# Eight output buffers, a tile table written in portions, and a weight load cut in five, in the first expert phase of a four-layer stack

## What is computed

```python
g = jnp.einsum('th,ehi->tei', x, w1)
u = jnp.einsum('th,ehi->tei', x, w3)
act = jax.nn.silu(g) * u
expert_out = jnp.einsum('tei,eih->teh', act, w2)
out = jnp.einsum('teh,te->th', expert_out, scores)
```

## Time and profile before

| what | us |
|---|---|
| median of 3 runs | 1810.74 (1809.96 to 1812.17) |
| the profiled execution | 1807.37 |
| its span on the core | 1805.5 |
| PE busy in the span | 1688.2 (93%) |
| DVE busy | 1149.0 (64%) |
| POOL busy | 912.8 (51%) |

### The profile page before, as it was taken

How to read it: one execution, slowest core, us unless ns; L and a number is a source line. 1 busy time by engine, 2 the same in 40 slices (tenths; PEclk the granted TensorE clock), 3 DMA queues, 4 the chain that set the end, 5 groups by cost and what they waited for, 6 DMA issues and landing times. The chain is left out here.

```text
span 1805.5 us, 38557 instructions
## 1 busy us (share of the span) xinstructions
PE 1688.2 (93%) x11984; PEld 1312.4 (73%) x12029; DVE 1149.0 (64%) x3410; ACT 974.7 (54%) x2775; POOL 912.8 (51%) x1088
## 2 busy tenths in 40 slices
PE   7999689989789999999999999999988999979997
PEld 4787468868646777777777777768867888847765
DVE  4787665638656666666666676457875453347765
ACT  4677245534335566566655666457761455536661
POOL 2366565545446555655565555134765344466610
PEclk9999899999999999999999999999999999999999
DMA  4233275565020000000000000022435344342101
GB/s 159 86 105 116 87 245 165 166 210 179 28 93 1 1 1 1 1 2 1 1 1 2 1 1 1 1 80 90 145 125 180 97 126 131 112 154 79 39 7 47
DMA packets 74549, 138.47 MB, mean 77 GB/s; under 512 B 11568, under 2 KB 56880, under 8 KB 71920
## 3 DMA queue, kind: packets, MB, share of 16 engines
q1 hardware_dynamic: 60624, 96.40, 17.1%
q0 software_dynamic: 13728, 39.60, 6.3%
HBM read 85.14 MB, written 50.82 MB: 75 GB/s over the span
## 5 line engine op out<-in xcount | busy, mean ns | idle before, releaser
L1404 POOL TENSOR_TENSOR L1f_rn<-L1f_ss,L1f_root_c 128x8 f32<-128x8 f32 x64 | 105.5, 1649 | 201.6 <-DVE L1f_ss L1710 199.3
L1537 PE MATMUL L1f_psQ<-L1f_xT,arena 128*128 128x128 f32 x1408 | 168.1, 275 | 0.9 <-ACT L1f_xT L1618 0.9
L1537 PEld LDWEIGHTS L1f_psQ<-L1f_xT,arena 128*128 128x128 f32 x1408 | 165.0, 192 | 3.0 <-ACT L1f_xT L1618 1.1
L2028 POOL DMA_INDIRECT outs_L2f<-L2f_tiles_ys,L2f_tiles_spot x79 | 75.7, 959 | 121.6 <-ACT L2f_tiles_ys L2172 116.1
L1419 POOL TENSOR_TENSOR L1f_rot<-L1f_qn,L1f_sinT 128x512 f32<-128x512 f32 x64 | 113.2, 1788 | 29.2 <-DVE L1f_qn L1726 29.2
L1636 ACT ACTIVATE L1f_sg<-L1f_psQ,vec1f 128x128 f32<-128x128 f32 x192 | 63.4, 364 | 119.0 <-PE L1f_psQ L1537 118.0
L1464 PE MATMUL L1f_psQ<-arena,L1f_hT 128*128 128x512 f32 x256 | 118.4, 605 | 0.6 <-ACT L1f_hT L1625 0.6
L1756 DVE SCALAR_TENSOR_TENSOR L1f_hid<-L1f_psQ,vec1f,L1f_sg 128x128 f32<-128x128 f32 x192 | 61.4, 346 | 78.1 <-ACT L1f_sg L1636 76.8
L2028 POOL DMA_INDIRECT outs_L0f<-L0f_tiles_ys,L0f_tiles_spot x79 | 75.8, 959 | 54.9 <-ACT L0f_tiles_ys L2172 49.0
L1549 PE MATMUL L1f_psB<-arena,L1f_hid 128*128 128x256 f32 (+1 forms) x384 | 99.8, 388 | 0.0
L1409 POOL TENSOR_TENSOR L1f_pr<-L1f_pr,L1f_rs 128x512 f32<-128x512 f32 x64 | 95.6, 1514 | 6.8 <-DVE L1f_rs L1720 6.8
(11 more groups left out here) (545 smaller groups left out, 4664.0 us busy)
## 6 DMA issues: line engine op xcount, KB each, us to landing
L0f_tiles_xs<-rows_L0f SPq DMA_DIRECT2D x79, 144.0 KB
L2f_tiles_xs<-rows_L2f SPq DMA_DIRECT2D x79, 144.0 KB, 2.2
arena<-in_w_L2f SPq DMA_DIRECT2D x8, 1120.0 KB, 5.6
arena<-in_w_L1f SPq DMA_DIRECT2D x8, 1088.0 KB, 7.4
L1x_got<-outs_L0f SPq DMA_DIRECT2D x16, 512.0 KB, 4.2
L3x_got<-outs_L2f SPq DMA_DIRECT2D x16, 512.0 KB, 3.4
arena<-in_w_L0f SPq DMA_DIRECT2D x8, 768.0 KB, 4.8
rows_L0f<-zero SPq DMA_DIRECT2D x31, 144.0 KB
```

Source lines behind the costliest of these rows:

```text
L1404: nc.gpsimd.tensor_tensor(rn[:, s.p, h], ss[:, s.p, h], root_c[:, 0:LH], ALU.pow).then_inc(s_rn, 1)
L1537: mm = nc.tensor.matmul(out, w, xT[:, k], start=(k == 0), stop=(k == KC - 1), skip_group_check=True)
L2028: nc.gpsimd.indirect_dma_start(r.outs, bass.IndirectOffsetOnAxis(spot[:, t % YR:t % YR + 1], 0), ys[:, t % YR], None).then_inc(r.s_out[t % ...
```

## The change

YR goes from 4 to 8, for both expert phases, with as many semaphores. The owners of the second list are worked out in four portions of 11 or 12 tiles, behind tiles 12, 14, 16 and 18, where one step stood behind tile 12. PE's turning of the table waits only for the links ahead of them (LISTED). The L2x weights go in four column slices of 512 (the last with 6 more) and the bias row as a fifth DMA, each behind the load of tile 40, 45, 50, 55 and 60. The L3x weights are cut in the same way, but all five DMAs are issued at the old place.

```diff
--- before.py
+++ after.py
@@ -66,7 +66,7 @@
 SPARE = TILES - FULL
 C_PAD = C_STEP + TILES
 CONSTS = C_PAD + TILES
-YR = 4
+YR = 8
 BATCHES = tuple((i, 2) for i in range(0, NB - 2, 2)) + ((NB - 2, 1), (NB - 1, 1))
 LASTS = [first + size - 1 for first, size in BATCHES]
 RING = 8
@@ -79,6 +79,9 @@
 
 COLS1X, ROWS1X = 4 * KC, 2 * D
 COLS1F, ROWS1F = 2 * KC + 2 * UNITS1, D + 2 * LD
+
+
+SLICES = {"L0x": 1, "L2x": 4, "L3x": 4}
 
 
 class Step:
@@ -216,7 +219,9 @@
 
         d = self.dram
         if name in ("L0x", "L2x", "L3x"):
-            return [(self.slot[:, 0:HEADS_W + 6], d[f"w_{name}"]),
+            n = HEADS_W // SLICES[name]
+            edges = list(range(0, HEADS_W, n)) + [HEADS_W + 6]
+            return [(self.slot[:, a:b], d[f"w_{name}"][:, a:b]) for a, b in zip(edges, edges[1:])] + [
                     (self.slot[:, HEADS_W + 6:SLOT], d[f"row_{name}"].partition_broadcast(P))]
         if name in ("L0f", "L2f"):
             n = (L0F if name == "L0f" else L2F) // 8
@@ -236,10 +241,11 @@
     def dma(self, eng, name, dst, src):
         eng.dma_start(dst, src).then_inc(self.loaded[name], 16)
 
-    def load(self, eng, name):
-
-        for dst, src in self.parts(name):
-            self.dma(eng, name, dst, src)
+    def load(self, eng, name, only=None):
+
+        for i, (dst, src) in enumerate(self.parts(name)):
+            if only is None or i == only:
+                self.dma(eng, name, dst, src)
 
     def load_in_rounds(self, eng, names, n):
 
@@ -253,7 +259,7 @@
 
     def wait(self, eng, name):
 
-        n = {"L0x": 2, "L2x": 2, "L3x": 2, "L0f": 8, "L2f": 8, "L1f0": 6, "L1f1": 6}.get(name, 3)
+        n = {"L0x": 2, "L2x": 5, "L3x": 5, "L0f": 8, "L2f": 8, "L1f0": 6, "L1f1": 6}.get(name, 3)
         eng.wait_ge(self.loaded[name], 16 * n)
 
 
@@ -1959,7 +1965,9 @@
     GROUPS = G if shared else 0
     READ, REST = r.ready, TILES - r.ready
     TABLE_AT, READ_ONE = 14, 3 if READ else 0
-    ALL_LINKS = TABLE_ROUTE + (READ_ONE + 6 if READ else 0)
+    OWNERS_AT = (12, 14, 16, 18)
+    LISTED = TABLE_ROUTE - 3 + (READ_ONE + 6 if READ else 0)
+    ALL_LINKS = LISTED + 3 * (len(OWNERS_AT) if READ else 1)
     with Phase(nc, r.name + "_tiles") as ph:
         xs, ys = ph.sb("xs", [P, XR, ROW]), ph.sb("ys", [P, YR, D])
         xT, sg, ac, aT = ph.sb("xT", [P, 2, D]), ph.sb("sg", [P, 2, P]), ph.sb("ac", [P, 2, W]), ph.sb("aT", [P, 2, W])
@@ -2014,9 +2022,9 @@
                 sp.dma_start(xs[:, t % XR], r.rows[bass.ds(row, P)]).then_inc(s_x[t % XR], 16)
                 if READ and XR <= t < XR + E:
                     empty(sp, [t - XR])
-                if READ and t == XR + E:
+                if READ and t > READ + XR and t % 5 == 0:
                     for load in loads:
-                        load(sp)
+                        load(sp, t // 5 - (READ + XR) // 5 - 1)
 
         @block.gpsimd
         def _(pool):
@@ -2039,7 +2047,7 @@
             cols = {}
 
             def table(bank):
-                pe.wait_ge(s_tab, ALL_LINKS)
+                pe.wait_ge(s_tab, LISTED)
                 for i in range(2):
                     mm = nc.tensor.transpose(psT[0:1, bank, i * P:(i + 1) * P], tab[:, 4 + i:5 + i], c.ident)
                 mm.then_inc(s_turned, 1)
@@ -2188,8 +2196,8 @@
             dve.wait_ge(r.s_place, 2 * len(BATCHES))
             v.tensor_scalar(r.ends[:, :], r.carry[0:1, len(BATCHES) % 2], -1.0, None, ALU.add).then_inc(s_ends, 1)
 
-            def owners(reached, lo, hi):
-                step = c.consts[:, C_STEP:C_STEP + hi - lo].unsqueeze(2).broadcast_to([P, hi - lo, E])
+            def owners(reached, lo, hi, base):
+                step = c.consts[:, C_STEP + lo - base:C_STEP + hi - base].unsqueeze(2).broadcast_to([P, hi - lo, E])
                 link(v.tensor_tensor(reach[:, lo:hi], reached.unsqueeze(1).broadcast_to([P, hi - lo, E]), step, ALU.is_gt))
                 link(v.tensor_copy(one[:, lo:hi, 0:1], reach[:, lo:hi, 0:1]), wait=False)
                 link(v.tensor_tensor(one[:, lo:hi, 1:], reach[:, lo:hi, 1:], reach[:, lo:hi, 0:E - 1], ALU.subtract), wait=False)
@@ -2231,19 +2239,20 @@
                 link(v.scalar_tensor_tensor(tab[:, 5:6], tab[:, 7:8], tab[:, 6:7], tab[:, 5:6], ALU.mult, ALU.add))
                 link(v.tensor_scalar(tab[:, 4:5], tab[:, 0:1], float(r.unit), None, ALU.mult))
 
-            def tile_owners():
-                owners(run2[:, :], READ, TILES)
-                assert link.n == ALL_LINKS
+            def tile_owners(i, n):
+                lo, hi = (READ + i * (TILES - READ) // n for i in (i, i + 1))
+                owners(run2[:, :], lo, hi, READ)
+                assert i + 1 < n or link.n == ALL_LINKS
 
             if READ:
-                owners(r.reached[:, :], 0, READ)
+                owners(r.reached[:, :], 0, READ, 0)
             else:
                 tile_counts()
                 sums()
                 experts()
                 tile_rows()
                 spare_rows()
-                tile_owners()
+                tile_owners(0, 1)
 
             def table(bank):
                 dve.wait_ge(s_turned, 1)
@@ -2325,8 +2334,8 @@
                     tile_rows()
                 if READ and t == 10:
                     spare_rows()
-                if READ and t == 12:
-                    tile_owners()
+                if READ and t in OWNERS_AT:
+                    tile_owners(OWNERS_AT.index(t), len(OWNERS_AT))
                 if turned_next and t in TURNS:
                     i = TURNS.index(t)
                     if i == 0:
@@ -2344,7 +2353,7 @@
         prepare(nc, c, dram)
 
         def loads(*names):
-            return [lambda sp, n=n: c.load(sp, n) for n in names]
+            return [lambda sp, only=None, n=n: c.load(sp, n, only) for n in names]
         with ExitStack() as first:
             r = Route(nc, first, ctx, "L0f", 1, 0, UNIT_GLU, False, READY)
             heads_attention(nc, c, "L0x", 0, mask=dram["mask"], loads=("L0f", "L1x"), route=r)
```

## The result

| what | before | after |
|---|---|---|
| median of 5 runs, us | 1809.96 (1805.83 to 1812.17) | 1801.03 (1799.15 to 1802.36) |
| ratio to before, 95% interval | | 0.9955 [0.9939, 0.9971] |
| the profiled execution, us | 1807.37 | 1800.39 |
| its span, us | 1805.5 | 1798.3 |

The change makes the kernel 8.9 us faster by the medians and 7.2 us by the spans. The interval of the ratio stands for a gain between 5.3 and 11.0 us. The forecast was 1802.3 with 8.4 us gained. The diff moves the code of expert_tiles down by eight or nine lines: silu is L2166, spot L2305, hidden L2100, turn_in L2088, the load of a tile L2022.

What follows compares the result with a forecast made beforehand. PE was taken to bound the first expert phase, with holes. Gains of 1.6 + 6.76 + 0.45 us, less 0.3 (row write) and 0.1 (load parts), gave 8.4 us off 1810.74: 1802.3 us, range 1799.5 to 1807.0.

Steps and rivals of the forecast that it cites:

- Eight buffers remove the waits for scatters: First expert phase: all 11 DVE waits for scatters, 12.3 us, should go; tiles 9 to 13 gain 1.6 us.
- the table steps: Tiles 9 to 13: DVE's table steps behind tiles 7, 8 and 10 stay and keep 0.45 us of the loss.
- The hole of 6.76 us: Tiles 22 and 23: scatter waits and lower clock go with eight buffers and the L2x load moved; gain 6.76 us.
- Parts of the L2x load: Behind tiles 40 to 60: each quarter delays the next load 1.4 us, which fits; 0.1 us lost for all five.
- rival 3: Tiles 41, 46, 51, 56: load parts delay tile loads beyond their free time, making the kernel slower, 1817.5 us; chance 0.05.
- The free time of a tile load: A tile's load has some 6.0 us from issue to use, 2.2 for landing, so 3.8 us are free.
- Owners in portions: Behind tiles 12 to 18: 0.32 us per large instruction, 3.0 us of DVE work instead of 2.0, cost 0.
- Tile 15: PE's turning of the table and DVE's copy wait for each other; untouched, gain 0, still 1.4 us lost.
- Tile 31 and the last row write: Tile 31's scatter wait goes, gain 0.45 us; last row write delays tile 32's load, issued at 276.1, costing 0.3.
- Rival 1: Tile 31: row-write chain takes over, PE waits up to 2.8 us, gain falls to some 5, 1805.5 us; chance 0.16.
- L3x: Before L2f: three DMAs more, 1.4 us of SP, hidden by 10 us of waiting for row writes; effect nothing.
- The rule on the shared port: DVE operations with two SBUF inputs lock out POOL; could cost up to 1.0 us, but nothing was charged.

Runs made afterwards that it cites:

- yr8_only: The kernel before with eight output buffers instead of four and nothing else: 1807.46 us against 1808.24, ratio 0.9993.
- no_move: The changed kernel with the L2x load back behind tile 22 and the L2x and L3x weights uncut: 1808.02 us, ratio 0.9998 to the kernel before.
- move_only: The changed kernel with four output buffers and owners in one piece, keeping the moved and cut loads: 1804.15 us, ratio 0.9977 to the kernel before.
- both_new_2: The changed kernel with earlier late row writes and the table turned into the other half of psT: 1801.83 us, ratio 0.9953 to the kernel before.
- no_yr8: The changed kernel with four output buffers instead of eight, owners still in portions: 1803.87 us, ratio 0.9975 to the kernel before.
- whole_at_40: The changed kernel with the L2x load uncut, all of it behind the load of tile 40: 1801.53 us, ratio 0.9949 to the kernel before.
- no_portions_2: The changed kernel with the owners in one piece behind tile 12: 1801.27 us against 1811.13 for the kernel before, ratio 0.9947.
- after_again: The changed kernel unchanged, on a slower chip: 1830.89 us, ratio 0.9987 to the kernel before.
- early_rows: The changed kernel with late row writes behind tiles 1, 3, ... 15 instead of 2, 5, ... 23, on the slower chip: 1831.78 us, ratio 0.9991.

## Why the prediction was right, point by point

- **Eight buffers remove the waits for scatters.** Shown: 12.3 us in 11 times to no row at all, and back to 8.9 us in 14 times when the buffers alone are undone. Tiles 9 to 13 gained 2.04 - 0.22 = 1.8 us, predicted 1.6. The 0.45 us left for the table steps was 0.22.
- **The hole of 6.76 us.** The prediction said that with eight buffers alone the load of tile 23 would still be late. Shown: 7.02 and 7.19 us lost with it in the old place. The gain was 6.76, as predicted. The prediction didn't say what each part carries: the move alone takes 4.9 to 6.1 us of it, the buffers alone nothing, and the buffers are needed only for the rest. With the hole the stretch at the lower clock went: the granted clock was 0.66 there in yr8_only and no_move too, with PE standing about 4 us at a time, and 1.00 in move_only, where it never stood so long.
- **Parts of the L2x load.** Predicted 0.1 us lost; measured 0.28 against 0.35 before in tiles 41 to 62, so nothing, and rival 3 with its four late loads didn't come. The estimate of 1.4 us delay for a part wasn't measured by itself.
- **The free time of a tile load.** This step is a figure for some tiles and not for all. I took 6.0 us from issue to use. At tile 40 it is 6.3, so the parts were costed rightly. At tile 22 it was 3.6, and by the 5.5 us of delay measured there I took the whole load for more than tile 40 could hide. It isn't: the delay was 6.5 - 2.2 = 4.3 us, 4.1 were free, and PE waited 0.16.
- **Owners in portions.** Predicted 0.32 us for a large instruction and cost 0; measured 0.32 to 0.40 us, and no loss is seen behind tiles 12 to 18. The reason that I gave for the part, that in one piece it might delay PE, isn't borne out: one piece costs nothing either.
- **Tile 15.** Predicted untouched, 1.4; measured 1.56. The wait is the turning of the table: with the other half of psT and one iteration more it fell to 0.26.
- **Tile 31 and the last row write.** The load of tile 32 was predicted for 276.1 and went out at 275.58; it took 3.1 us and not 2.2, so PE waited 0.49 us, and the tile lost 0.87 in this profile, 0.45, 0.46 and 1.15 in three others with the same row writes. Predicted was 0.3 us of stall in place of the 0.45 that goes, so the term is too small by 0.15 to 0.85 us. The 0.45 was misread as well. The prediction counted it as one of the eleven waits for scatters, but it doesn't go with them: with eight buffers, no wait for a scatter and the L2x load in its old place tile 31 still loses 0.38 (yr8_only) and 0.50 us (no_move). So the gain of 0.45 in the sum isn't borne out. In yr8_only PE stands before hidden of tile 31, right behind the turning of tile 32, for nothing that the profile shows:

```profile
287.02 0.73 PEld L2092 LDWEIGHTS L0f_tiles_psH<-arena,L0f_tiles_xT 128*128 128x128 f32 x4 [0.35 <-issue]
```

The chain, row write, load, PE, stands in the timeline; the one test of it on such a chip, both_new_2 with the row writes earlier, has no loss at tile 31. Since no_yr8 has none either, with the old places, one profile isn't proof. Rival 1, a stall of up to 2.8 us, was of the right kind and too large.

- **L3x.** Predicted nothing. The phase of L2f comes 6.5 us earlier (first tile load at 1384.6, before 1391.1) and is no longer: 173.9 us from the first to the last load, before 174.6. Of the 8.0 us by which silu of tile 78 comes earlier, 1.5 are lost again before L2f and 0.7 gained in it, which gives the 7.2 us of the spans. From silu of tile 78 to the first load of L2f the profiles on the faster chips take 1025.9 to 1029.9 us, in no order of the edits, so that much of a difference between two executions has nothing to do with the change.

```profile
L2022 SPq DMA_DIRECT2D L2f_tiles_xs<-rows_L2f x79: 332/333/346, 1384.6 to 1558.5; - x79
```

- **Tile 20, not foreseen.** The changed kernel loses some 0.5 us there, in two profiles. In the timeline PE's hidden of that tile begins late, after a wait that the profile ties to nothing:

```profile
260.31 1.12 PE L2100 MATMUL L0f_tiles_psH<-arena,L0f_tiles_xT 128*128 x4 [0.27 <-issue]
```

It isn't in whole_at_40 (0.06), which has the same owners, and in no_portions_2, without a portion there, 0.28 us are lost. So the portions don't explain it. This stays open.

By steps: 1.8 and 6.76 us gained, less 0.1 (tile 15), 0.5 (tile 20), 0.4 (tile 31) and 0.1 in small change between, give the 7.43 us to a rounding of tiles 8 to 78. Silu of tile 78 comes 365.22 - 357.19 = 8.0 us earlier; the 0.6 us between was gained before tile 8. The beginning of the phase varies that much by itself: silu of tile 2 lies between 228.80 and 231.10 us in the profiles on the faster chips, in no order of the edits. The forecast's median had 8.4 us of gain for 8.9 measured. That this is so near is in part luck. Between tiles 8 and 78 the sum was 1.0 us too high (8.4 against 7.43): 0.6 us at tile 31, 0.5 at tile 20 and 0.3 at tile 15 and between, less 0.4 that tiles 9 to 13 and the load parts did better. That the medians gained more than the 7.2 us of the two profiled executions is within what executions of one kernel differ by. The main term, the hole, was right by its mechanism and its size.

The rule on the shared port (the Trainium skill, SBUF — State Buffer, "SBUF: two separate sides") is narrower on the page than the prediction has it: an operation with two SBUF inputs counts only against a GpSimd operation that reads SBUF. The scatters read their rows and row numbers from SBUF tiles (ys and spot), so the rule would have shown as longer scatters on POOL beside DVE's comparisons. All 79 scatters of the changed kernel:

```profile
L2036 POOL DMA_INDIRECT outs_L0f<-L0f_tiles_ys,L0f_tiles_spot x79: 954/959/987, 230.9 to 361.4; - x79
```

954 to 987 ns, with a median of 959, leaves no room for an instruction held up for 0.3 us. Four of them ran at the same time as one of the comparisons of 0.34 to 0.40 us, and took 0.95 or 0.96 us. For indirect DMAs on POOL beside such DVE instructions the rule isn't seen here.

## What to carry to other kernels

When a timeline shows a wait, look for the next one that ends at the same place before pricing its removal: here two waits of 4.5 and 3.9 us lay on each other. Taking away the longer one alone, by buffers, gave nothing that could be told (0.02 and 0.07%). Moving the load that causes both gave 0.23 and 0.25%, and with the buffers 0.45%. So look for what the waits have in common, and move that first. A large load that isn't urgent belongs where the loads behind it have the most time between issue and use, and that time is read at the place itself (3.6 us beside the zero writes, 6.3 later in the same loop). With the place right, cutting it made no difference that could be measured.

## What the runs showed that I had not expected

**A chip that is 23 to 30 us slower.** From 600 to 1000 us, the local attention, it works as the others (PE busy 400.00 of 400 us in both). In the expert phase engines stand for times that no wait explains, in the waits of 225 to 375 us of after_again:

```profile
DVE L0f_tiles_ac L2287 <- issue: 14.7, 22, 2.8
ACT L0f_tiles_sg L2166 <- issue: 12.9, 18, 2.0
PEld L0f_tiles_psH L2100 <- issue: 10.2, 12, 1.9
...
ACT L0f_tiles_sg L2166 <- remote: 7.2, 4, 2.0
```

In the kernel after on the first chip, PEld's for hidden is 2.0 us in 4 times, and DVE and ACT have no such row for these two lines. The time is lost in steps: of 2.08 us at tile 7, 2.0 at 10, 2.06 at 19, 2.03 at 25 and 1.41 at 28, with smaller ones at 4, 14, 15, 22 and 23. That is the rhythm of the row writes behind tiles 2, 5, ... 23. In early_rows, with them behind every second tile up to 15, the steps come at tiles 4, 6, 8, 10, 12, 14, 15, 18 and 20, of 0.7, 3.5, 0.7, 3.5, 0.8, 3.1, 1.3, 3.5 and 0.8 us (0.9 us come back behind two of them), and from tile 21 on there are none to speak of before 54. So between tiles 3 and 53 the stops keep to the stretch of the row writes. They aren't all of it: of the 30.2 us by which the span of after_again is longer than that of the changed kernel on the first chip, 8.2 stand before silu of tile 8, 9.6 between tiles 8 and 78, 10.5 from there to the first tile load of L2f, and 2.4 in L2f. What in a row write brings them about there, and on the other chips not, wasn't found. In 225 to 375 us POOL's own row writes take 956 to 970 ns on this chip, 956 to 963 on the first.

The change was worth 0.13% there (0.9987 [0.9974, 1.0001], an interval that includes 1), against 0.45 and 0.50% on the others. That the waits it removes lie in those stops there would explain it; the kernel before wasn't profiled on that chip, so this is only argued.
